# Two attention stages of a decoder put into one order of work, with shared PSUM banks

## The reference, cut to what matters

```
def cross(x, cond):                      # 8 batches, 112 tokens, 375 text rows
    q, k, v = x @ w_q, cond @ w_k, cond @ w_v     # 16 heads of 64
    attn = softmax(q k^T * 64 ** -0.5)
    return (attn v) @ w_out + b_out
x = layernorm(x + cross(x, ctx_768))

def last(x):
    h = rms(x, n1_w)
    q, k = rms(heads(wq), qn_w), rms(heads(wk), kn_w)     # 16 heads of 16
    v = heads(wv)
    attn = softmax(causal(q k^T * 16 ** -0.5))
    ao = (attn v) @ wo.T;  ao[:, :, :64] = 0
    x = x + ao
    xf = rms(x, n2_w)
    wts = top-2 of softmax(xf @ gate_w.T)
    moe = sum of wts[:, e] * expert_e(xf), e = 0..3;  moe[:, :, :64] = 0
    return x + moe
x = layernorm(x + last(x))
```

## Time and profile before

| | us |
|---|---|
| median of 3 runs | 1377.57 (1368.01 to 1383.83) |
| the profiled execution | 1375.38 |
| its span, first to last instruction | 1373.6 |
| busy PE / PEld / DVE / ACT / POOL | 1092.5 / 762.3 / 692.9 / 581.6 / 277.6 |
| mean granted clock of TensorE | 0.894 |

### The profile page before, as it was taken

How to read it: one execution, slowest core, us unless ns; L and a number is a source line. 1 busy time by engine, 2 the same in 40 slices (tenths; PEclk the granted TensorE clock), 3 DMA queues, 4 the chain that set the end, 5 groups by cost and what they waited for, 6 DMA issues and landing times.

```text
span 1373.6 us, 20562 instructions
## 1 busy us (share of the span) xinstructions
PE 1092.5 (80%) x8144; PEld 762.3 (56%) x8144; DVE 692.9 (50%) x1616; ACT 581.6 (42%) x1349; POOL 277.6 (20%) x282
## 2 busy tenths in 40 slices
PE   6988588776776787879999768787888486778996
PEld 3676356554446776435565456565666254453764
DVE  3323456632654774364655337575775445636203
ACT  4311146651244653334444325444554144447542
POOL 2401213100040000521111210020001634124443
PEclk9966769988787999899999989999999788789998
DMA  8410324500465770642221046633430000000000
GB/s 295 101 24 0 92 61 102 113 10 0 161 213 184 243 305 13 216 131 84 96 93 62 23 140 229 189 91 91 111 93 1 0 1 1 1 1 1 1 1 27
DMA packets 66591, 123.61 MB, mean 90 GB/s; under 512 B 11536, under 2 KB 42224, under 8 KB 62416
## 3 DMA queue, kind: packets, MB, share of 16 engines
q1 hardware_dynamic: 63728, 117.48, 28.2%
q0 software_dynamic: 1536, 3.67, 0.9%
q10 hardware_dynamic: 1232, 1.15, 0.3%
HBM read 86.30 MB, written 35.92 MB: 89 GB/s over the span
## 4 chain that ended last, share of the span: by engine, by line
PE 54%; DVE 21%; ACT 13%; POOL 4%; DMA 4%; issue 4%; SPq 0%; DVEq 0%; ACTq 0%
PE psum L369 42%; ACT s_p L2214 4%; DVE s_p L2260 2%; POOL rs L2647 2%; DVE s_max L1249 2%; DMA values<-s_v 2%; PE psum L1106 2%; PE psum L1134 2%; DVE s_max L2249 2%; PE psum L2179 1%; PE psum L2168 1%; DVE wu L1079 1%; DVE wd L1079 1%; PE psum L1886 1%; PE psum L2458 1%
## 5 line engine op out<-in xcount | busy, mean ns | idle before, releaser
L592 POOL TENSOR_TENSOR rstd<-meanvar,minus_half 112x1 f32<-112x1 f32 x40 | 23.4, 586 | 527.9 <-DVE meanvar L573 527.8
L2214 ACT ACTIVATE s_p<-psum,s_max 112x375 f32<-112x375 f32 x128 | 72.3, 569 | 78.4 <-DVE s_max L2249 78.4
L1249 DVE TENSOR_REDUCE s_max<-psum 112x2 f32<-112x750 f32 x64 | 60.0, 937 | 38.0 <-PE psum L1106 37.1
L369 PE MATMUL psum<-Wv,ctx 128*125 128x512 f16 x240 | 64.5, 429 | 8.0 <-ACT s_v L552 3.9
L2249 DVE TENSOR_REDUCE s_max<-psum 112x1 f32<-112x375 f32 x128 | 63.7, 539 | 0.9 <-PE psum L2160 0.9
L369 PE MATMUL psum<-ctx,Wk 128*128 128x375 f16 x320 | 61.5, 331 | 1.9 <-DVE s_k L582 1.5
L1198 ACT ACTIVATE s_pT<-psum 125x672 f32<-125x672 f32 x64 | 46.8, 731 | 36.0 <-PE psum L1122 34.7
L369 PE MATMUL psum<-x_ch,w_Wq 128*128 128x224 f32 x192 | 49.6, 395 | 15.3 <-DVE s_q L2236 7.5
L2957 POOL TENSOR_TENSOR hidden<-raw,hidden 128x448 f16<-128x448 f32 x44 | 46.7, 1061 | 64.5 <-ACT hidden L2840 62.9
L2533 ACT ACTIVATE sc<-psum,mx 112x112 f32<-112x112 f32 x128 | 34.5, 358 | 59.2 <-DVE mx L2602 59.1
L552 ACT ACTIVATE s_v<-psum 125x512 f32<-125x512 f32 x48 | 28.4, 597 | 72.8 <-PE psum L369 47.8
(11 more groups left out here) (352 smaller groups left out, 2638.3 us busy)
## 6 DMA issues: line engine op xcount, KB each, us to landing
keys<-s_k SPq DMA_DIRECT2D x64, 187.5 KB, 2.2
s_k<-keys SPq DMA_DIRECT2D x8, 1500.0 KB, 8.1
values<-s_v SPq DMA_DIRECT2D x48, 224.0 KB
s_v<-values SPq DMA_DIRECT2D x16, 672.0 KB
raw_wg<-in_wg SPq DMA_DIRECT2D x8, 1024.0 KB, 5.0
raw_wu<-in_wu SPq DMA_DIRECT2D x8, 1024.0 KB, 5.5
raw_wd<-in_wd SPq DMA_DIRECT2D x8, 1024.0 KB, 6.1
s_kd<-k_halves SPq DMA_DIRECT2D x48, 93.8 KB, 3.7
```

What stands on the lines that cost most here:

```text
L369: ins = TE.matmul(bank, left, right, start=i == 0, stop=last)
L1249: VE.tensor_reduce(s1_max[b % 2][:, 2 * p:2 * p + 2], rings["s1"][unit][0:N, :, 0:S], X, ALU.max, negate=True).then_inc(*V.up("max1", n))
L2214: SC.activation(rings["p4"][2 * n + j], rings["s4"][(n, j)][0:N, 0:S], ACT.Exp, bias=s4_max[b % 2][:, h:h + 1], accum_out=s4_sum[b % 2][:, ...
```

## The change

Stage 5's plan is gone: its streams are woven with those of stage 4 and there is no fence between them. Operands of the causal attention come from one stream, heads from one stream that goes through all batches (one group of 4 heads in up to four turns: s5e, s5, pT5, av5), outputs from two. Units that waited on another engine are cut in two (qkv5 and qkv5e, s5 and s5e, rms5a and ms5a), so that the second half stands later in the plan. Buffers of stage 5 go from four to two (q5, k5, v5, qk5, at5) or three (sc5, pT5). Six banks are shared by everything (s4, t4, misc4 and misc5 are one Ring, w4), o4 and o5 have one each; until_banks holds a stream until enough of the six are free in the plan. ACT copies q and k out of the bank (one more operation for a batch), and DVE scales them in SBUF. The experts' weights now lie where stage 4 had its buffers: they are fetched in three groups after the last av4 (ffnin), in order of use; e0_up, e1_w1 and e1_w2 are split before the experts start.

```diff
@@ -2044,16 +2044,22 @@
     wts.restart()
     ffn_w = {}
     late = Region(nc, ringm.base + 40 * KB, 8 * KB)
-    g_w5, g_w5b = Group("dma_w5"), Group("dma_w5b")
+    g_w5 = Group("dma_w5")
     for name, shape in (("wq5", [P, KC, D]), ("wk5", [P, KC, D]), ("wv5", [P, KC, D]),
                         ("wo5", [P, KC, KEPT]), ("gate5", [P, KC, E1])):
-        ffn_w[name] = g_w5.load(late if name != "gate5" else wts, name, shape)
-    for name, shape in (("e0_up", [P, KC, HID]), ("e1_w1", [P, KC, HID]), ("e1_w2", [P, KC, HID]),
-                        ("e2_l1", [P, KC, HID]), ("e2_l2", [P, HT, HID]), ("e2_l3", [P, HT, HID]),
-                        ("e3_down", [P, KC, D]), ("e3_up", [P, KC, HID]), ("e0_down", [P, HT, KEPT]),
-                        ("e1_down", [P, HT, KEPT]), ("e2_l4", [P, HT, KEPT]),
-                        ("e3_out", [P, HT, KEPT])):
-        ffn_w[name] = g_w5b.load(wts, name, shape)
+        ffn_w[name] = g_w5.load(late, name, shape)
+    ffn_m = Region(nc, work.base, work.size)
+    ffn_groups = [Group(f"dma_ffn{i}") for i in range(3)]
+    ffn_group = {}
+    for group, things in zip(ffn_groups, (
+            (("e0_up", [P, KC, HID]), ("e1_w1", [P, KC, HID]), ("e1_w2", [P, KC, HID])),
+            (("e0_down", [P, HT, KEPT]), ("e1_down", [P, HT, KEPT]), ("e3_down", [P, KC, D]),
+             ("e3_up", [P, KC, HID])),
+            (("e2_l1", [P, KC, HID]), ("e3_out", [P, HT, KEPT]), ("e2_l2", [P, HT, HID]),
+             ("e2_l3", [P, HT, HID]), ("e2_l4", [P, HT, KEPT])))):
+        for name, shape in things:
+            ffn_w[name] = group.load(ffn_m, name, shape)
+            ffn_group[name] = group
...
-    rings.update(s4=banks(0, 3), t4=banks(3, 2), o4=banks(5, 1), misc4=banks(6, 2),
-                 p4=Ring(s4_p), pT4=Ring(s4_pT))
+    k5 = [wts.tensor(f"k5_{i}", [P, KC, HPT, N]) for i in range(2)]
+    sq5 = wts.tensor("sq5", [N, 2 * D])
+    qk5 = [wts.tensor(f"qk5_{i}", [N, 2 * D]) for i in range(2)]
+    v5 = [wts.tensor(f"v5_{i}", [N, H, 2 * DH]) for i in range(2)]
+    junk5 = wts.tensor("junk5", [N, D])
+    at5 = [wts.tensor(f"at5_{i}", [N, D]) for i in range(2)]
+    sc5 = [ringm.tensor(f"sc5_{i}", [N, 4, N])[:] for i in range(3)]
+    pT5 = [ringm.tensor(f"pT5_{i}", [N, 4 * N])[:] for i in range(3)]
+    w4 = banks(0, 6)
+    rings.update(s4=w4, t4=w4, misc4=w4, misc5=w4, o4=banks(6, 1), o5=banks(7, 1),
+                 p4=Ring(s4_p), pT4=Ring(s4_pT), sc5=Ring(sc5), pT5=Ring(pT5))
...
+    step("ms5a", "V msa5, V epsa5, G rsa5")
+    step("qkv5", "T qk5, T v5", "misc5", "A qk5", 2600)
+    step("qkv5e", "A sq5, A qk5, A v5")
...
+    def until_banks(count):
+        while sum(all(name in r.value for r, name in freed) for freed in w4.freed) < count + 3:
+            yield None
...
-        if b == 4:
+        if b == 3:
             place(("n15",))
+            place(("ones5",))
...
+        place(("ffnin",))
...
+    def s5_operands(b):
+        yield from until(("norm", 4, b), ("ones5",))
+        if b >= 2:
+            yield from until(("turn5", b - 2))
+        yield [("rms5a", b)]
+        yield [("ms5a", b)]
+        yield from until(("xTe", 4, b))
+        yield from until_banks(2)
+        rings["misc5"].take(("vv5", b), (A, ("v5", b)))
+        yield [("qkv5", b)]
+        yield [("qkv5e", b)]
+        yield [("ms5", b)]
+        yield from rest(5000.0)
+        yield [("qk5", b)]
+        yield from rest(REST)
+        yield from until_banks(1)
+        yield [("qkT5", b)]
+        yield [("qkT5e", b)]
+    def s5_heads():
+        n, live = 0, []
+        while n < 4 * B or live:
+            b, g = divmod(n, 4)
+            start = n < 4 * B and (g > 0 or ("qkT5e", b) in placed
+                                   and (b < 2 or ("atT5e", b - 2) in placed))
+            if not start and not live:
+                yield None
+                continue
+            for at in [at for at, age in live if age == 1]:
+                yield [("s5e", *at)]
+            if start:
+                yield from until_banks(1)
+                rings["sc5"].take((b, g), (T, ("pT5", b, g)))
+                yield [("s5", b, g)]
+            for at in [at for at, age in live if age == 2]:
+                rings["pT5"].take(at, (T, ("av5", *at)))
+                yield [("pT5", *at)]
+            for at in [at for at, age in live if age == 3]:
+                if at[1] == 0:
+                    rings["o5"].take(at[0], (A, ("oT5", at[0])))
+                yield [("av5", *at)]
+                if at[1] == 3:
+                    place(("oT5", at[0]))
+            live = [(at, age + 1) for at, age in live if age < 3] + [((b, g), 1)] * start
+            n += start
+    def s5_out(b):
+        yield from until(("oT5", b))
+        yield from rest(REST / 2)
+        yield [("turn5", b)]
+        yield from rest(REST)
+        yield from until_banks(1)
+        yield [("atT5", b)]
+        yield [("atT5e", b)]
+        yield from rest(REST)
+        yield [("wo5", b)]
+        yield from rest(REST / 2)
+        yield [("sqb5", b)]
+        yield from rest(REST / 2)
+        yield [("msb5", b)]
+        yield from rest(REST_POWER)
+        yield [("xf5", b)]
+        yield from rest(REST)
+        yield from until_banks(1)
+        yield [("xfT5", b)]
+        yield [("xfT5e", b)]
+    def s5_split():
+        yield from until(("qkT5e", B - 1))
+        yield split5(w16_m, "e0_up")
+        yield from until(("s5e", B - 1, 3))
+        yield split5(w16_m, "e1_w1")
+        yield split5(w16_m, "e1_w2")
...
+          follow(s5_operands, range(B)), s5_heads(), follow(s5_out, range(0, B, 2)),
+          follow(s5_out, range(1, B, 2)),
+          s5_split())
...
+            elif what == "ffnin":
+                sp.wait_ge(T["av4", B * HP - 1])
+                for group in ffn_groups:
+                    group.start()
...
-    xf = work.tensor("xf", [P, KC, T_])
-    xf16 = ringm.tensor("xf16", [P, 2, KC, T_], F16)
...
-    rings.update(misc5=banks(0, 6), o5=banks(6, 2), sc5=Ring(sc5), pT5=Ring(pT5))
...
-    def s5_operands(b):
-        if b >= 4:
-            yield from until(("turn5", b - 4))
-        yield [("rms5a", b)]
-        rings["misc5"].take(("vv5", b), (A, ("v5", b)))
-        yield [("qkv5", b)]
-        yield from rest(REST_POWER + 2 * H * POWER_NS)
-        yield [("qk5", b)]
-        yield from rest(REST)
-        yield [("qkT5", b)]
-        yield from rest(REST / 2)
-        yield [("qkT5e", b)]
-    def s5_heads(b):
-        yield from until(("qkT5e", b))
-        if b >= 4:
-            yield from until(("atT5e", b - 4))
-        rings["o5"].take(b, (A, ("oT5", b)))
-        for g in range(6):
-            if g < 4:
-                rings["sc5"].take((b, g), (T, ("pT5", b, g)))
-                yield [("s5", b, g)]
-            if 1 <= g <= 4:
-                rings["pT5"].take((b, g - 1), (T, ("av5", b, g - 1)))
-                yield [("pT5", b, g - 1)]
-            if g >= 2:
-                yield [("av5", b, g - 2)]
-            else:
-                yield None
-        yield [("oT5", b)]
-        yield from rest(REST / 2)
-        yield [("turn5", b)]
-    def s5_out(b):
-        yield from until(("turn5", b))
-        yield from rest(REST)
-        yield [("atT5", b)]
-        yield from rest(REST / 2)
-        yield [("atT5e", b)]
-        yield from rest(REST)
-        yield [("wo5", b)]
-        yield [("rms5b", b)]
-        yield from rest(REST_POWER)
-        yield [("xf5", b)]
-        yield from rest(REST)
-        yield [("xfT5", b)]
-        yield [("xfT5e", b)]
-    def s5_split():
-        yield from until(("atT5e", 3))
-        yield split5(Region(nc, ringm.base + ringm.at, 4 * KB), "e0_up")
-    place(("ones5",))
-    weave(*(follow(s5_out, range(j, B, 2)) for j in range(2)),
-          *(follow(s5_heads, range(j, B, 2)) for j in range(2)),
-          *(follow(s5_operands, range(j, B, 4)) for j in range(4)), s5_split())
...
+            SC.activation(sq5[:], ring[("qkv5", b)][0:N, :], ACT.Square).then_inc(*A.up("sq5", b))
+            SC.activation(qk5[b % 2][:], ring[("qkv5", b)][0:N, :], ACT.Copy).then_inc(*A.up("qk5", b))
...
+            dve.wait_ge(G["rs5", b], A["qk5", b])
+            VE.tensor_tensor(heads_of(qk5[b % 2][:], DH), heads_of(qk5[b % 2][:], DH),
...
-        for region, names in ((free_m, ("e1_w1", "e1_w2", "e0_down", "e1_down", "e2_l1", "e2_l2",
+        for region, names in ((w16_m, ("e0_down", "e1_down")),
+                              (w16_w, ("e3_down", "e3_up", "e2_l1", "e3_out", "e2_l2", "e2_l3",
+                                       "e2_l4"))):
```

More of the change, by code:

```diff
@@ L2077, in build @@
     step("q4", "T q4, A q4, V q4", "misc4", "V q4", 750)
+    step("ffnin")
+    step("ones5", "V +1, V v1s5, G +3, G mask5")
+    step("rms5a", "G xin5, A sqa5")
+    step("ms5a", "V msa5, V epsa5, G rsa5")
+    step("qkv5", "T qk5, T v5", "misc5", "A qk5", 2600)
+    step("qkv5e", "A sq5, A qk5, A v5")
+    step("ms5", "V +1, V ms5, G rs5")
```

(72 more changed lines are left out.)

518 lines of the change are left out of this document (245 added, 273 removed).

## The result

The change made the kernel slower: 1408.18 us median of 4 (1400.55 to 1409.84) against 1372.79 (1361.40 to 1383.83), ratio 1.0275, 95% interval 1.0186 to 1.0364. Forecast were 1313 us with 1272 to 1352 and a chance of 0.85 for faster. The prediction was wrong in sign, and the time lies outside its range. The profiled execution took 1408.81 us, its span 1407.0.

A forecast was written before the change was run, and what follows sets the result against it. PE was taken as busiest, with gaps from DVE and ACT under head pairs and chains binding the stretch before the experts. Span 1373.6 + 43 - 103 - 3 = 1310.6 us, with overheads 1313; range 1272 to 1352.

The forecast's parts named there:

- stretch A: Head pairs of the wide-headed attention: 234.7 us grow to 278 (+43) as causal work moves in; bounds 258 and 300.
- Rival one: Shared banks make head pairs a lockstep, scores waiting for the previous pair's second exponential: 394 us there, 1446 whole; chance 0.08.
- What lands under the head pairs: Count of turns: heads of four causal batches and operands, 51 us of PE work, move there; four batches of heads stay behind.
- B: Last output projection to first expert product: 172.6 us shrink to 70 (-103), four batches left; bounds 50 and 88.
- C: Experts, 150.3 us now: two weight splits fewer save 3 us; bounds 0 and 6.
- The weights: Experts' weights, 6.55 MB, fetched after the last av4 in 21 us, in time for first use 44 us after; no gain.
- Rival four: Under head pairs, five POOL powers of 5.4 us each block DVE whole: +27 us, 1340 whole; chance 0.03.

The follow-up runs named there:

- freed_first: Changed kernel, same order of units; each takes the shared bank whose freeing result was placed longest ago, not the one taken longest ago: 1351.19 us, ratio 0.9811.
- apart: Changed kernel with the causal attention's streams in a second weave behind the head pairs, nothing mixed, no fence: 1400.16 us, ratio 1.0144.
- freed_last: Kernel before, six banks shared by head pairs, transposes and other stage 4 products, each unit taking the bank freed last: 1667.70 us, ratio 1.2067.

## Why the prediction was wrong, point by point

**The step that failed** is the sum of stretch A, "195.4 + 51 = 246 us of PE work. To that come gaps": 32 us of gaps at a clock near 1. The PE work was about right: busy time by clock is 301.8 x 0.84 = 254 us after, 272.2 x 0.92 = 250 in freed_first (an estimate, as the clock is a mean). That has some luck in it: 22 groups came under the head pairs where I had counted 16, each for less than my price. So 385 us are 250 of work, some 50 for the slow clock and 83 of gaps. I sized the gaps by what stands in order on ACT and DVE and left out which bank a unit gets; and I had a slow clock only in the tail. The row that could have warned me is the earlier trace rows: after 4.20 us without work the four transposes take 1.00 us, and 0.59 otherwise. With the banks given in order of their freeing and k5 at a distance, A is 295.7 us, inside my bounds of 258 to 300. Of the 107 us by which A exceeded 278, the banks give back 66 and the distance 23; the 18 left weren't taken apart.

**Rival one** had the direction and nearly A's length (394, measured 385; it decided from 340), at a chance of 0.08. Part of that is luck, as it had another place, 22 groups beside the 16 of the main count, and 90 us for what its own terms make 97 (22 x 4.4); its whole was 1446, measured 1408. Its place was wrong: I looked at the second exponential of the pair before, whose banks cost 3.0 us. The ring was a lockstep through the banks that the causal units hold over several turns. I argued it away with the 0.9 us that PE has more in a step, without going through the order in which six banks come round.

**What lands under the head pairs.** 22 groups of 32 are placed before the last av4, not 16; DVE's row of their maxima shows them:

```profile
L2647 DVE TENSOR_REDUCE mx<-psum 112x4 f32<-112x448 f32 x22 | 13.7, 624 | 53.7 <-PE psum L369 53.7
```

The first group came where I had it (pair 23, my round 48), but two batches took 17 pairs, 34 rounds, where I had counted 43.

**B was right by luck, from two errors that cancel.** 67.2 against 70: 2.5 batches at about 20 us each, not four at 14 to 15. The chain was summed at 14 us and takes 16 in apart; that the next batch's products begin 4 us late, behind scores that wait, wasn't in it. Once the products are in front, the batches come at 15.9.

**C**: 149.6 against 150.3, so the two splits gave 0.7 us and not 3.

**The weights** were right. After the last av4 they come at 337 to 433 GB/s, 6.55 MB within some 18 us; the first split starts at 1230.9, 40 us after (44 forecast), and no PE wait names them:

```profile
GB/s 0 36 376 337 344 378 409 433 423 428 409 78 5 0 0 0 0 0 0 0 0 9 0 0 0 0 0 0 0 0 0 0 0 0 0 0 0 0 0 0
...
q1 hardware_dynamic: 1728, 6.55, 23.6%
```

**Rival four** (a power blocks DVE whole) didn't occur. Beside the power that POOL begins at 926.00 (5.43 us), the scaling is as long as in the earlier trace rows:

```profile
928.93 0.74 DVE L2412 TENSOR_SCALAR s_p<-s_p,s_sum 112x375 f32<-112x375 f32 x2
929.58 1.00 DVE L2401 TENSOR_REDUCE s_max<-psum 112x1 f32<-112x375 f32 x2
```

## What to carry to other kernels

Where buffers are handed out in a plan that engines run in order, "free in the plan" isn't free on the chip: choose the buffer whose freeing result was placed longest ago, not the one taken longest ago, as soon as some are held over several units. When work is merged under other work, go through the buffers for one full turn and price each gap of PE twice, once as a wait and once as slower work after it. And look at what stands on the busiest engine behind a unit that waits: moving the next batch's products in front of such a wait, with a rest before the scores, took 33 us off 190.

## What the runs showed of the hardware

The granted clock can fall with gaps of under a microsecond when there are many: in freed_last, waits of 0.8 us on average in front of most units went with a clock of 0.58, near the level of 1.2 GHz, though PE was busy in 67% of the stretch by its rows. The Trainium skill, TensorE: Matmul & The Clock Gate, section A second HAM failure mode: psum-queue depth-cycling, tells of a kernel whose clock went back and forth because PE idled shortly between groups while cycling through PSUM banks; the traces here agree, with 0.99, 0.92, 0.84 and 0.58 in A as the bank waits grow. The Trainium skill, Perfetto Trace Analysis, section Matmuls, advises to let independent groups rotate through different banks; the changed kernel did rotate, and freed_first shows that the turn in which they rotate is worth 66 us of A.

Useless products in such gaps can be worth their time: 21 us of them, by the forecast's 0.87 us each, made the tail 10 us shorter.

A DVE operation with both inputs in SBUF was slowed by POOL. The scaling of q and k takes 0.68 us in the changed kernel while POOL does nothing. In apart it took 1.21 us while POOL added two SBUF tiles (0.72 us, begun 0.06 before), in three batches alike:

```profile
1138.64 0.72 POOL L2702 TENSOR_TENSOR x_tok<-x_tok,x_in 112x256 f32<-112x256 f32 x1
1138.70 1.21 DVE L2632 TENSOR_TENSOR qk<-qk,rs 112x512 f32<-112x512 f32 x1 [2.06 <-POOL rs L2694]
```

That is 0.53 us longer, where a full block until POOL's end would be 0.66. Beside a copy of 0.40 us on POOL it took 0.86 us in two batches (0.18 longer, a full block 0.32), and beside the power of one column (0.55 us) 0.69 us in three, no longer than alone. The Trainium skill, SBUF - State Buffer, section Who interferes with whom, has a DVE instruction with two SBUF inputs as one that contends with a GpSimd instruction that reads SBUF; these rows agree in kind, but the delay is less than a block for the whole POOL row, and none beside the small power. The rows named in the prediction for this rule, are of a DVE operation with one tile and a column of sums, so they don't settle it for two tiles. The power of 32 columns itself can't meet this operation here, which waits for it.
